# The last mixture's gate per half, its rows kept by expert and its first block by a 0/1 product; both mixtures' closing additions on two engines and an early first down product

## The chip, the cores and the metric

The kernel runs on one core of one Trainium2 chip. The metric is the device time of one execution, in microseconds (us). All arrays are float32 unless a line says otherwise.

## The reference

1024 tokens (32 x 32) of width 256 pass through four layers; each layer adds cross attention, attention and a feed-forward part, each of the layer-normed tokens. The change touches the feed-forward parts of the last two layers, both mixtures of eight experts of which every token takes two. The last one, cut:

```python
gates = softmax(x @ Wg + bg)
_, top_idx = top_k(gates, 2)
mask = one_hot(top_idx, 8).sum(axis=-2)
g = gates * mask
g = g / maximum(sum(abs(g)), 1e-12)
h = gelu(einsum('btd,edh->bteh', x, W1) + b1)      # 256 -> 1024
eo = einsum('bteh,ehd->bted', h, W2) + b2          # 1024 -> 256
return einsum('bte,bted->btd', g, eo)
```

The one before it, the capacity mixture, uses relu and gives each expert at most 160 tokens, the first in token order that chose it.

## The kernel before, in words

`program` (3284) runs the parts as stages one after another, with a barrier of all engines between two. The tokens stay in SBUF as `core.x`, 8 tiles of 128 tokens. Each engine has its own instruction stream and executes it in order; waits on semaphores are written out by hand, and that order is what this change is about. DMAs are issued by SP (most), ACT (its own queue) and POOL (indirect ones).

**The scan** (`stage_scan`, 1835) is the stage ahead of the capacity mixture. At its start SP issues its own loads and then `cw.sp` (2170): it fills the capacity mixture's DRAM arrays `moecap_xin` and `moecap_acc` with neutral rows from the input `nobody` and loads the weights of three experts.

**The capacity mixture** (`stage_moe_capacity`, 2276). `Norm` (74) normalizes in two halves of four tiles; PE turns tiles, ACT copies them to `xnT`. `TopTwo` (2177) computes the two largest gates of a half: PE's logits, twelve small DVE steps each waiting for the one before it (`Chain`, 61), and on PE the rank of each token within its expert (`rank`, 2221, bf16 products of the 0/1 mask with an upper triangle and with ones). The local `slots(h)` (2491) turns ranks into row numbers; POOL scatters the rows of the half to `moecap_xin` (L2364). The first expert doesn't wait for the scatter: DVE builds a 0/1 matrix (L2520, `onehot`), and PE multiplies the tokens with it (`dispatch`, L2387). Experts then go through `turn_x` (L2397), `up` (L2407), ACT's `relu` (L2473), `down` (L2417) and `turn_y` (L2428); in the loop before, the order on PE is up(0), turn_x(1), up(1), turn_x(2), down(0), up(2), ... Results go by POOL's indirect DMA to `moecap_acc` (L2370). At the end SP and ACT fetch both contributions of each tile (`bring`, 2325), and DVE adds share times contribution to `core.x`, two operations for each of eight tiles (L2556).

**The last attention** (`stage_attn3`, in `stage_one_head`, 1354). Its SP calls `ew.sp` (2577): first the whole of `moe_xin` is filled from `nobody` (L2578, 2944 rows), then the 16 MB of the last mixture's weights follow (L2580, L2581).

**The last mixture** (`stage_moe`, 2584). SP issues the small loads (2657 to 2663); ACT waits for all of them before its first copy. `Gate` (2065) works on all eight tiles at once: logits (L2094), softmax, `max` and `max_index` per tile, mask, weights. DVE then sums the masks (L2807), PE forms ranks (L2703 to L2705), and DVE computes how many blocks of 128 rows each expert needs, where each expert's rows begin, and the row of each token (L2816 to L2828). Rows are packed: expert e begins at the block where expert e - 1 ends, and 23 blocks cover every case. POOL scatters 16 times 128 rows to `moe_xin` (L2686). Meanwhile DVE builds the table `expert_u` of the expert of each block, PE turns the weights of the tokens (L2708) and multiplies them with `b2` (L2714), and DVE adds this to `core.x` (L2843).

The loop over blocks: SP loads block n (L2669) into one of two buffers `x_slots`; for n of 2 and more it first waits until block n - 2 is turned and its row numbers are copied (`row_ready`, L2668). `expert_of` (2642) reads the expert's number from SBUF into a register. PE's iteration n is turn_x(n + 1) (L2723), up(n) (L2735, in two halves), down(n - 1) (L2745). DVE's iteration n is prepare(n + 1) (b1 of the expert, L2849, and the block's row numbers, L2851), weights(n + 1) (two copies of W1's halves to `w1_now`, L2859, each after the half of up(n) that used the place), taken(n - 1) (L2865). ACT applies gelu (L2789), POOL writes results to `moe_acc` (L2691). At the end `bring` (L2653), sixteen DVE additions (L2881), and eight stores of the tiles (L2674). A line on DVE, before:

```python
for n in range(BLOCKS + 1):
    if n + 1 < BLOCKS:
        prepare(n + 1)
        weights(n + 1)
    if n:
        taken(n - 1)
```

Of the kernel before, what the change touches and what calls it, by code (L numbers as in the profile page):

```python
# [6 lines left out]
ALU = mybir.AluOpType  # L7
# [7 lines left out]
P = 128  # L15
# [1819 lines left out]
def stage_scan(core, cw):  # L1835
# [11 lines left out]
    with ExitStack() as ctx:  # L1847
# [44 lines left out]
        def _(sp):  # L1892
# [9 lines left out]
            cw.sp(sp)  # L1902

# [161 lines left out]
class Gate:  # L2065


    def __init__(self, st, experts, wg, bg, logits):
        self.core, self.E, self.wg_dram, self.bg_dram, self.logits = st.core, experts, wg, bg, logits
        full = [P, TILES, experts]  # L2070
        self.wg, self.bg = st.sb("gate_w", [P, CD, experts]), st.sb("gate_b", [P, experts])
        self.number = st.sb("gate_number", [P, experts])
        self.sub, self.probs, self.mask = st.sb("gate_sub", full), st.sb("gate_probs", full), st.sb("gate_mask", full)
        self.second, self.weight = st.sb("gate_second", full), st.sb("gate_weight", full)
        self.most, self.total = st.sb("gate_most", [P, TILES]), st.sb("gate_total", [P, TILES])
        self.top, self.index = st.sb("gate_top", [P, TILES, 8]), st.sb("gate_index", [P, TILES, 8], U32)
        self.place = st.sb("gate_place", [P, TILES, 8])
        self.loaded = st.sem("gate_loaded")
        self.logits_done, self.sub_ready = st.sem("gate_logits_done"), st.sem("gate_sub_ready")
        self.exp_ready, self.ready = st.sem("gate_exp_ready"), st.sem("gate_ready")  # L2080

    def sp(self, sp):
        sp.dma_start(self.wg[:, :, :], self.wg_dram.rearrange("(c p) e -> p c e", p=P)).then_inc(self.loaded, 16)  # L2083
        sp.dma_start(self.bg[:, :], self.bg_dram.partition_broadcast(P)).then_inc(self.loaded, 16)
        sp.dma_start(self.number[:, :], self.core.dram["number"][0:self.E].partition_broadcast(P)).then_inc(self.loaded, 16)

    def pe(self, pe):

        core, nc = self.core, self.core.nc
        pe.wait_ge(self.loaded, 48)  # L2090
        for t in range(TILES):
            out = self.logits[:, t * self.E:(t + 1) * self.E]
            for c in range(CD):
                mm = nc.tensor.matmul(out, core.xnT[:, c, t * P:(t + 1) * P], self.wg[:, c, :], start=(c == 0), stop=(c == CD - 1))  # L2094
        mm.then_inc(self.logits_done, 1)

    def act(self, act):
        act.wait_ge(self.sub_ready, 1)
        self.core.nc.scalar.activation(self.probs[:, :, :], self.sub[:, :, :], ACT.Exp).then_inc(self.exp_ready, 1)

    def dve(self, dve, step):
        nc, full = self.core.nc, [P, TILES, self.E]
        by_token = lambda a: a.unsqueeze(2).broadcast_to(full)
        dve.wait_ge(self.loaded, 48)
        dve.wait_ge(self.logits_done, 1)
        step(nc.vector.tensor_tensor(self.sub[:, :, :], self.logits.rearrange("p (t e) -> p t e", t=TILES),
                                     self.bg[:, :].unsqueeze(1).broadcast_to(full), ALU.add))
        step(nc.vector.tensor_reduce(self.most[:, :], self.sub[:, :, :], AX.X, ALU.max))
        nc.vector.tensor_tensor(self.sub[:, :, :], self.sub[:, :, :], by_token(self.most[:, :]), ALU.subtract).then_inc(self.sub_ready, 1)
        dve.wait_ge(self.exp_ready, 1)  # L2110
        step(nc.vector.tensor_reduce(self.total[:, :], self.probs[:, :, :], AX.X, ALU.add))
        step(nc.vector.reciprocal(self.total[:, :], self.total[:, :]))
        step(nc.vector.tensor_tensor(self.probs[:, :, :], self.probs[:, :, :], by_token(self.total[:, :]), ALU.mult))
        for t in range(TILES):
            step(nc.vector.max(self.top[:, t, :], self.probs[:, t, :]))  # L2115
        for t in range(TILES):
            step(nc.vector.max_index(self.index[:, t, :], self.top[:, t, :], self.probs[:, t, :]))  # L2117
        step(nc.vector.tensor_copy(self.place[:, :, :], self.index[:, :, :]))
        number = self.number[:, :].unsqueeze(1).broadcast_to(full)
        step(nc.vector.tensor_tensor(self.mask[:, :, :], number, by_token(self.place[:, :, 0]), ALU.is_equal))  # L2120
        step(nc.vector.tensor_tensor(self.second[:, :, :], number, by_token(self.place[:, :, 1]), ALU.is_equal))
        step(nc.vector.tensor_tensor(self.mask[:, :, :], self.mask[:, :, :], self.second[:, :, :], ALU.add))
        step(nc.vector.tensor_tensor(self.weight[:, :, :], self.probs[:, :, :], self.mask[:, :, :], ALU.mult))
        step(nc.vector.tensor_reduce(self.total[:, :], self.weight[:, :, :], AX.X, ALU.add))
# [3 lines left out]
        dve.sem_inc(self.ready, 1)  # L2128

# [1249 lines left out]
```

## Time and profile before

| | us |
|---|---|
| median of 3 runs | 2022.66 (2016.35 to 2028.9) |
| profiled execution | 2018.47 |
| its span in the profile | 2016.6 |
| PE busy | 1633.3 (81%) |
| DVE busy | 1173.3 (58%) |
| ACT busy | 867.7 (43%) |
| POOL busy | 711.4 (35%) |

PE is TensorE's products, PEld its weight loads (they overlap), DVE VectorE, ACT ScalarE, POOL GpSimd, SPq the queue of SyncE. Busy shares are averages over stages with different limits. In timelines a row is: start in us from the span's start, duration in us, engine, line, operation, written tensor, read tensors, shapes, count; in square brackets the idle time of the engine ahead of it and what ended that. The granted clock of TensorE is a share of full speed (1.00 is 2.4 GHz, 0.50 is 1.2 GHz).

### The profile page before, as it was taken

The page shows a single profiled execution, that of the slowest core. Times are in us where ns is not written, and L with a number is a line of the kernel's source. Part 1 is how long each engine was busy: PE and PEld are TensorE (multiplying, and loading weights), DVE is VectorE, ACT ScalarE, POOL GpSimd, SP SyncE. Part 2 cuts the span into 40 slices and gives each one's busy share as a digit, 9 for nine tenths or more (in the row PEclk, how much of TensorE's full clock was granted, in tenths as well). Part 3 has the DMA queues.
Part 4 walks back from the last instruction along what each step waited for, and adds up shares of the span by engine and source line. Part 5 has one row for each costly group of instructions (what it writes and reads, how often), then busy time and mean ns, then how long its engine had stood idle before and what let it go on. Part 6 is the DMA issues. An engine that isn't in the chain of part 4 may idle for free. (4 is left out here: it accounts for less than half of the span.)

```text
span 2016.6 us, 36051 instructions
## 1 busy us (share of the span) xinstructions
PE 1633.3 (81%) x12690; PEld 1402.0 (70%) x12690; DVE 1173.3 (58%) x3187; ACT 867.7 (43%) x2475; POOL 711.4 (35%) x780
## 2 busy tenths in 40 slices
PE   6999998650785999977999999699595388757996
PEld 6988997330465999946899889456494266546996
DVE  5666665688774888835666666289413565442222
ACT  4666664114543888812666666200131133112332
POOL 7655552541116999713000000177312211112111
PEclk9999999885896999987999999799697588858998
DMA  8444441010004333205222222520362210931112
GB/s 249 149 148 148 149 148 67 29 39 5 0 1 132 130 134 133 94 16 169 75 93 93 93 93 75 165 95 1 91 202 62 68 52 28 320 119 56 38 38 81
DMA packets 120795, 195.52 MB, mean 97 GB/s; under 512 B 17672, under 2 KB 87408, under 8 KB 120272
## 3 DMA queue, kind: packets, MB, share of 16 engines
q1 hardware_dynamic: 113504, 181.32, 27.3%
q0 software_dynamic: 3408, 8.54, 1.2%
q10 hardware_dynamic: 3712, 3.41, 0.6%
q8 instruction: 103, 1.69, 0.3%
q14 instruction: 68, 0.56, 0.1%
HBM read 154.16 MB, written 45.52 MB: 99 GB/s over the span
## 5 line engine op out<-in xcount | busy, mean ns | idle before, releaser
L672 DVE TENSOR_SCALAR xattn_oT<-bank,xattn_last 128x256 f32<-128x256 f32 x256 | 111.7, 478 | 100.1 <-PE bank L512 100.1
L592 ACT ACTIVATE xattn_probs<-bank,xattn_negmax 128x257 f32<-128x257 f32 x256 | 124.2, 485 | 57.8 <-DVE xattn_negmax L653 57.8
L653 DVE TENSOR_REDUCE xattn_negmax<-bank 128x1 f32<-128x257 f32 x256 | 108.0, 422 | 63.0 <-PE bank L485 61.3
L597 ACT ACTIVATE xattn_probs<-xattn_probs,xattn_rsum 128x257 f32<-128x257 f32 x256 | 131.9, 515 | 1.4 <-DVE xattn_rsum L657 1.4
L832 POOL TENSOR_SCALAR xattn_probs<-xattn_probs,xattn_rsum 128x257 f32<-128x257 f32 x128 | 119.9, 937 | 22.9 <-DVE xattn_rsum L1067 22.7
L1907 POOL MEMSET scan_decay<- 128x64 f32 x1 | 0.2, 214 | 337.1 <-POOLq L51 337.1
L603 ACT CAST xattn_probsT_hi<-bank 128x256 fp32r<-128x256 f32 x256 | 95.7, 374 | 40.4 <-PE bank L492 36.7
L662 DVE TENSOR_TENSOR xattn_probsT_lo<-bank,xattn_probsT_hi 128x256 fp32r<-128x256 f32 x256 | 104.9, 410 | 8.3 <-ACT xattn_probsT_hi L603 7.2
L492 PE MATMUL bank<-ident,xattn_probs 128*128 128x128 f32 x512 | 103.6, 285 | 2.5 <-ACT xattn_probs L597 2.0
L136 PE MATMUL bank<-ident,xn 128*128 128x128 f32 x144 | 32.6, 406 | 90.0 <-DVE xn L112 90.0
L481 PE MATMUL bank<-xattn_ctxT,xattn_qk_hi 128*128 128x258 f32 x256 | 93.6, 366 | 0.5 <-DVE xattn_qk L649 0.5
L136 PEld LDWEIGHTS bank<-ident,xn 128*128 128x128 f32 x144 | 26.8, 211 | 95.6 <-DVE xn L112 95.2
L507 PE MATMUL bank<-xattn_probsT_hi,xattn_ctxN 128*128 128x256 f32 x256 | 85.2, 333 | 5.0 <-DVE xattn_oT L672 3.4
L1920 POOL TENSOR_TENSOR scan_product<-scan_state,scan_qT 128x512 f32<-128x512 f32 x64 | 75.7, 1183 | 36.6 <-DVE scan_state L2057 36.2
L2735 PE MATMUL bank<-moe_xinT,moe_w_now 128*128 128x128 f32 x736 | 87.6, 278 | 0.3 <-DVE moe_w_now L2859 0.3
L2735 PEld LDWEIGHTS bank<-moe_xinT,moe_w_now 128*128 128x128 f32 x736 | 85.6, 195 | 0.7 <-ACT moe_xinT L2779 0.6
L402 POOL TENSOR_SCALAR xattn_ctxT<-xattn_rawT 128x514 fp32r<-128x514 f32 x32 | 48.4, 1511 | 102.9 <-issue 101.9
L463 PE MATMUL bank<-xattn_qT,xattn_wk 64*128 64x128 f32 x1024 | 73.3, 283 | 12.8 <-DVE xattn_qT L638 10.0
L2745 PE MATMUL bank<-moe_w,moe_hT 128*128 x368 | 83.1, 379 | 0.0
L2057 DVE TENSOR_TENSOR_SCAN scan_state<-bank,scan_decay 128x264 f32<-128x264 f32 x128 | 81.3, 688 | 1.3
L528 PE MATMUL bank<-xattn_oT,xattn_wv 128*64 128x128 f32 x1024 | 70.7, 282 | 10.0 <-issue 7.6
L463 PEld LDWEIGHTS bank<-xattn_qT,xattn_wk 64*128 64x128 f32 x1024 | 62.2, 187 | 21.9 <-issue 12.6
(500 smaller groups left out, 5426.1 us busy)
## 6 DMA issues: line engine op xcount, KB each, us to landing
xattn_ctxT<-ctx_partsT SPq DMA_DIRECT2D x64, 516.0 KB, 3.6
xattn_ctxN<-ctx_partsN SPq DMA_DIRECT2D x64, 384.0 KB, 3.1
ctx_partsT<-xattn_ctxT SPq DMA_DIRECT2D x32, 516.0 KB, 3.0
moe_w<-in_L_ffn_W SPq DMA_DIRECT2D x16, 1024.0 KB, 13.9
ctx_partsN<-xattn_ctxN SPq DMA_DIRECT2D x32, 384.0 KB, 3.9
moecap_w_early<-in_L_ffn_w SPq DMA_DIRECT2D x10, 1024.0 KB, 12.7
xattn_rawN<-in_ctx SPq DMA_DIRECT2D x32, 192.0 KB
moecap_w_late<-in_L_ffn_w SPq DMA_DIRECT2D x6, 1024.0 KB, 7.5
```

Source lines behind the costliest of these rows:

```text
L463: mm = nc.tensor.matmul(bank[:, k * P:(k + 1) * P], wk_s[r, h // 2, g % 2 * P:(g % 2 + 1) * P], qT[r, h // 2, :], start=True, stop=True, t ...
L481: nc.tensor.matmul(out, unit(qk1[0]), part(0, 0), start=True, stop=False)
L492: mm = nc.tensor.transpose(TB[n % 2][:, c * P:(c + 1) * P], probs[:, n % RING, c * P:(c + 1) * P], core.ident[:, :])
L507: nc.tensor.matmul(OB[:, 0:2 * P], first_hi(c), hi[:, c], start=(c == 0), stop=False)
L592: nc.scalar.activation(probs[:, n % RING, :], SB[n % 2][:, 0:KV], ACT.Exp, bias=negmax[:, n % RING:n % RING + 1], accum_out=psum[:, n % RI ...
L597: nc.scalar.mul(probs[:, n % RING, :], probs[:, n % RING, :], rsum[:, n % RING:n % RING + 1]).then_inc(norm_ready, 1)
L603: nc.scalar.copy(probsT[0][:, n // 2 % PAIRS, :, n % 2, :], TB[n % 2][:, 0:2 * P].rearrange("p (c n) -> p c n", c=2)).then_inc(probsT_hi_r ...
L653: nc.vector.tensor_reduce(negmax[:, n % RING:n % RING + 1], SB[n % 2][:, 0:KV], AX.X, ALU.max, negate=True).then_inc(negmax_ready, 1)
L662: nc.vector.tensor_tensor(lo, TB[n % 2][:, 0:2 * P].rearrange("p (c n) -> p c n", c=2), hi, ALU.subtract).then_inc(probsT_ready, 1)
L672: nc.vector.tensor_scalar(oT[k][:, heads, b, :], by_head(OB[:, k * 2 * P:(k + 1) * 2 * P]), last[:, k, j * PER_TILE + b:j * PER_TILE + b + ...
L832: nc.gpsimd.tensor_scalar(probs[:, n % RING, :], probs[:, n % RING, :], rsum[:, n % RING:n % RING + 1], None, ALU.mult).then_inc(norm_read ...
L2735: mm = nc.tensor.matmul(H[n % 2][k][:, f * P:(f + 1) * P], w1_now[:, c, at:at + P], xinT[:, n % 2, c, :], start=(c == 0), stop=(c == CD - 1))
```

## The change

In the scan SP issues one more DMA, `er.sp`: it fills all of `moe_xin`, which now has a region of 1024 rows for each expert (9088 rows instead of 2944). The fill in `ew.sp` goes. A token's row is its rank in the expert plus 1024 times the expert, so it doesn't depend on how full the others are; a second table `block_row_u` gives the first row of each block, and SP reads from it. The last mixture uses `TopTwo` in halves and scatters in halves; its first block (expert 0) comes from a 0/1 product; down(0) and the b2 shares stand behind up(0). In the capacity mixture down(0) stands behind up(0). In both, ACT scales and POOL adds three of the eight closing tiles. `class Gate` is removed. The diff, cut:

```diff
+BY_POOL = (0, 3, 6)
+BY_DVE = tuple(t for t in range(TILES) if t not in BY_POOL)
...
     def rank(self, pe, h, out, count=None):
...
+        if count is not None:
+            for t in range(TILES):
+                mm = nc.tensor.matmul(count, self.up_to_b[:, 1, :], self.mask[:, t, :], start=(t == 0), stop=(t == TILES - 1))
```

The capacity mixture on PE:

```diff
             for n in range(E + 2):
                 if n < E:
                     up(n)
+                if n == 0:
+                    down(0)
                 if n + 1 < E:
                     turn_x(n + 1)
                 if n >= 2:
                     turn_y(n - 2)
-                if 1 <= n <= E:
+                if 2 <= n <= E:
                     down(n - 1)
```

Both mixtures, the ends of ACT, POOL and DVE, and the fill of `moe_xin`:

```diff
+            act.wait_ge(shares_ready, 1)
+            for t in BY_POOL:
+                act.wait_ge(brought[t], TOP * 16)
+                for k in range(TOP):
+                    nc.scalar.mul(mine[k][:, t, :], mine[k][:, t, :], share[:, k, t:t + 1]).then_inc(scaled, 1)
...
+            for n, t in enumerate(BY_POOL):
+                for k in range(TOP):
+                    pool.wait_ge(scaled, n * TOP + k + 1)
+                    if k:
+                        pool.wait_ge(pool_added, n * TOP + k)
+                    nc.gpsimd.tensor_tensor(core.x[:, t, :], core.x[:, t, :], mine[k][:, t, :], ALU.add).then_inc(pool_added, 1)
...
-            for t in range(TILES):
+            for n, t in enumerate(BY_DVE):
...
+class ExpertRows:
+    def sp(self, sp):
+        sp.dma_start(self.core.moe_xin, self.core.dram["nobody"]).then_inc(self.core.moe_cleared, 16)
...
 class ExpertWeights:
     def sp(self, sp):
-        sp.dma_start(self.xin, self.d["nobody"]).then_inc(self.cleared, 16)
```

The last mixture on SP:

```diff
+        def row_of(eng, n):
+            return eng.value_load(block_row_u[0:1, n:n + 1], min_val=0, max_val=xin.shape[0] - P) if n else 0
...
-            sp.dma_start(up_to[:, :, :], d["up_to"]).then_inc(loaded, 16)
+            sp.dma_start(place[:, :], d["number"][1:P + 1].partition_broadcast(P)).then_inc(loaded, 16)
...
+            sp.wait_ge(experts_ready, 1)
             sp.wait_ge(scattered, TILES * TOP * 16)
             for n in range(BLOCKS):
                 if n >= XS:
                     sp.wait_ge(x_turned, n - XS + 1)
                     sp.wait_ge(row_ready, n - XS + 1)
-                sp.dma_start(x_slots[:, n % XS, :], xin[n * P:(n + 1) * P, :]).then_inc(x_loaded[n % XS], 16)
+                sp.dma_start(x_slots[:, n % XS, :], xin[bass.ds(row_of(sp, n), P), :]).then_inc(x_loaded[n % XS], 16)
```

The last mixture on PE (`shares_of_b2` holds the turns of the weights and the b2 products, which stood ahead of the loop before):

```diff
             def up(n):
                 pe.wait_ge(xT_ready, n + 1)
+                if n == 1:
+                    pe.wait_ge(b2_added, TILES // 2)
...
+            dispatch()
+            pe.wait_ge(ew.loaded, E * 32)
+            up(0)
+            down(0)
+            shares_of_b2()
             pe.wait_ge(experts_ready, 1)
-            pe.wait_ge(b2_added, TILES // 2)
-            pe.wait_ge(ew.loaded, E * 32)
-            turn_x(0)
-            for n in range(BLOCKS + 1):
+            turn_x(1)
+            for n in range(1, BLOCKS + 1):
                 if n + 1 < BLOCKS:
                     turn_x(n + 1)
                 if n < BLOCKS:
                     up(n)
-                if n:
+                if n >= 2:
                     down(n - 1)
```

The last mixture on DVE (`slots(h)` waits for the ranks of the half, adds `begins`, multiplies with the two picks, sums, casts to `slot_u`, signals `slots_ready` and forms `in_first`, 6 steps):

```diff
+            for h in range(2):
+                gate.dve(dve, step, h)
+                slots(h)
+            nc.vector.tensor_tensor(onehot, in_first[:, :].unsqueeze(2).broadcast_to(shape), place[:, :].unsqueeze(1).broadcast_to(shape),
+                                    ALU.is_equal).then_inc(onehot_ready, 1)
...
             prepare(0)
             weights(0)
+            tables()
+            weights_of_tokens()
             for n in range(BLOCKS + 1):
                 if n + 1 < BLOCKS:
                     prepare(n + 1)
                     weights(n + 1)
+                if n == 0:
+                    add_b2()
+                if n < BLOCKS:
+                    row(n)
                 if n:
                     taken(n - 1)
```

`row(n)` holds the two lines that leave `prepare(n)`: the wait for the block's rows and the copy of their row numbers (`row_ready`). `tables()` is the arithmetic for `expert_u` and `block_row_u` (15 steps), `weights_of_tokens()` the shares and the token weights (6 steps). On ACT the order is turned_x(0), gelu(0), the copies of the turned weights, turned_x(1), and then turned_x(n + 1), gelu(n) as before. POOL issues eight scatters after `slots_ready` 1 and eight after 2.

## Rows read from the trace of the kernel before

**Rows 1.** Stretch: length, busy us (count) of five engines, PE clock, DMA share, GB/s

```profile
1831.00:1994.00 163.00, 162.74 (x1124) 152.90 (x1124) 45.17 (x111) 61.87 (x207) 20.13 (x21) 0.99 0.11 35
```

**Rows 2.** Chain of waits that ended last, last mixture (start, us, what)

```profile
1777.44 3.85 DMA moe_b<-in_L_ffn_b
...
1825.21 2.43 DMA moe_xin<-moe_x,moe_slot_u
...
1827.66 2.00 DMA moe_x_slots<-moe_xin
...
1830.44 0.70 DVE moe_w_now L2859
...
1836.85 3.57 PE bank L2735 x32
```

**Rows 3.** DMA issues: count, KB each, median us to landing

```profile
moe_xin<-in_nobody SPq DMA_DIRECT2D x1, 2955.5 KB, 11.7
```

**Rows 4.** A stretch (columns as in rows 1) and the first issue of the last mixture

```profile
1765.00:1770.00 5.00, 4.49 (x23) 3.38 (x21) 2.52 (x6) 1.88 (x6) 0.00 (x0) 1.00 1.06 379
...
1770.80 1.87 SPq L2083 DMA_DIRECT2D moe_gate_w<-in_L_ffn_Wg  x1
```

**Rows 5.** Timeline of the capacity mixture (start, us, engine, line, op)

```profile
1422.61 0.60 SPq L2338 DMA_DIRECT2D moecap_b<-in_L_ffn_b_cols  x1
...
1425.56 0.30 ACT L2446 COPY moecap_x<-moecap_rows 128x8 f32<-128x8 f32 x2 [107.42 <-DMA moecap_b<-in_L_ffn_b_cols]
...
1437.58 1.22 POOL L2364 DMA_INDIRECT moecap_xin<-moecap_x,moecap_slot_u  x1 [11.36 <-issue]
...
1443.04 1.49 DVE L2520 TENSOR_TENSOR xnT<-moecap_chosen,moecap_place 128x1280 f32<-128x1280 f32 x1
...
1444.58 6.67 PE L2387 MATMUL bank<-xnT,moecap_x 128*128 128x160 f32 x32 [4.61 <-DVE xnT L2520]
...
1451.87 4.58 PE L2407 MATMUL bank<-moecap_xinT,moecap_w_early 128*128 128x160 f32 x32 [0.61 <-ACT moecap_xinT L2466]
...
1463.77 0.80 PE L2397 MATMUL bank<-ident,moecap_x_slots 80*128 80x80 f32 x4 [7.32 <-DMA moecap_x_slots<-moecap_xin]
...
1465.13 6.63 PE L2407 MATMUL bank<-moecap_xinT,moecap_w_early 128*128 128x160 f32 x32 [0.56 <-issue]
...
1476.26 4.51 PE L2407 MATMUL bank<-moecap_xinT,moecap_w_early 128*128 128x160 f32 x32
```

**Rows 6.** Timeline of one block of the last mixture

```profile
1967.14 3.74 PE L2735 MATMUL bank<-moe_xinT,moe_w_now 128*128 128x128 f32 x32
...
1967.98 0.15 DVE L2851 CAST moe_row_u<-moe_x_slots 128x1 uint32<-128x1 f32 x1
...
1968.20 0.32 SPq L2669 DMA_DIRECT2D moe_x_slots<-moe_xin  x1
...
1970.72 3.62 PE L2745 MATMUL bank<-moe_w,moe_hT 128*128 x16
...
1971.03 0.69 DVE L2859 COPY moe_w_now<-moe_w 128x1024 f32 x1 [1.09 <-PE bank L2735]
...
1974.17 0.38 PE L2723 MATMUL bank<-ident,moe_x_slots 128*128 128x128 f32 x2
```

**Rows 7.** Value loads, line 2643: duration ns min/median/max

```profile
L2643 DVEq TENSOR_LOAD <-moe_expert_u x46: 298/304/552, 1810.8 to 1982.4; - x46
```

**Rows 8.** Stretches when PE ran dry at the end, columns as in rows 1

```profile
1999.00:2000.00 1.00, 0.31 (x2) 0.00 (x0) 0.42 (x1) 0.00 (x0) 0.00 (x0) 1.00 0.01 0
...
2001.00:2002.00 1.00, 0.00 (x0) 0.00 (x0) 0.00 (x0) 0.00 (x0) 0.49 (x1) 0.89 0.00 0
```

**Rows 9.** Closing additions: last one on DVE; an addition of this shape on POOL

```profile
2013.29 0.48 DVE L2881 SCALAR_TENSOR_TENSOR x<-xnT,moe_share,x 128x256 f32<-128x256 f32 x1
...
L3018 POOL TENSOR_TENSOR x<-x,xattn_bo x8: 724/728/734, 1598.7 to 1603.5; 128x256 f32<-128x256 f32 x8
```

More of the change, by code:

```diff
@@ L2061, in _ @@
                 add(t, bank[t - len(OUT)])
[L2065 to L2090, printed above, removed]
-        for t in range(TILES):
[L2092 to L2124, printed above, removed]
-        step(nc.vector.tensor_scalar(self.total[:, :], self.total[:, :], 1e-12, None, ALU.max))
-        step(nc.vector.reciprocal(self.total[:, :], self.total[:, :]))
-        step(nc.vector.tensor_tensor(self.weight[:, :, :], self.weight[:, :, :], by_token(self.total[:, :]), ALU.mult))
-        dve.sem_inc(self.ready, 1)
@@ L2220, in pe, with rank @@
         mm.then_inc(self.logits_done, 1)
-    def rank(self, pe, h, out):
+    def rank(self, pe, h, out, count=None):
         nc, E, first = self.core.nc, self.E, h * 4
@@ new lines, in _, with dispatch @@
+            for h in range(2):
+                gate.rank(pe, h, RANK[h], COUNT if h else None)
+            def dispatch():
+                pe.wait_ge(onehot_ready, 1)
+                for c in range(CD):
+                    for t in range(TILES):
+                        mm = nc.tensor.matmul(XT[0][:, c * P:(c + 1) * P], xk[0][:, t, c * P:(c + 1) * P], onehot[:, t, :],
+                                              start=(t == 0), stop=(t == TILES - 1))
+                mm.then_inc(x_turned, 1)
@@ L2797, in _ @@
             bring(act, 1)
+            act.wait_ge(shares_ready, 1)
+            for t in BY_POOL:
+                act.wait_ge(brought[t], TOP * 16)
+                for k in range(TOP):
+                    nc.scalar.mul(mine[k][:, t, :], mine[k][:, t, :], share[:, k, t:t + 1]).then_inc(scaled, 1)
         @block.vector
@@ L2802, in _ @@
             step = Chain(dve, steps)
-            gate.dve(dve, step)
-            tiles = [P, TILES, E]
-            step(nc.vector.memset(before[:, 0, :], 0.0))
-            for t in range(TILES):
-                add = nc.vector.tensor_tensor(before[:, t + 1, :], before[:, t, :], gate.mask[:, t, :], ALU.add)
-                if t < TILES - 1:
-                    step(add)
-            add.then_inc(before_ready, 1)
-            step(nc.vector.tensor_tensor(first[:, :, :], gate.mask[:, :, :], gate.second[:, :, :], ALU.subtract))
@@ new lines, in weights_of_tokens, with add_b2 @@
+            def weights_of_tokens():
+                gate.shares(dve, step)
+                dve.sem_inc(shares_ready, 1)
+                for k in range(TOP):
+                    step(nc.vector.tensor_tensor(chosen[:, k, :, :], gate.picked[:, k, :, :], share[:, k, :].unsqueeze(2).broadcast_to([P, TILES, E]), ALU.mult))
+                nc.vector.tensor_tensor(weight[:, :, :], chosen[:, 0, :, :], chosen[:, 1, :, :], ALU.add).then_inc(weight_ready, 1)
+            def add_b2():
+                for k in range(TILES // 2):
+                    dve.wait_ge(b2_done, k + 1)
+                    both = core.x[:, 2 * k:2 * k + 2, :].rearrange("p t n -> p (t n)")
+                    nc.vector.tensor_tensor(both, both, bank[k], ALU.add).then_inc(b2_added, 1)
```

211 lines of the change are left out of this document (122 added, 89 removed).

## Prediction

> **What bounds the kernel now.** I read the busy shares of the page first, then the stretches, then the chain of waits of the last mixture, then the timelines of both mixtures. The change touches only the two mixtures, one DMA in the scan, and nothing of the other 1,600 us. In the main loop of the last mixture PE is busy 162.7 of 163 us at a granted clock of 0.99 [rows 1]: there only less PE work, or a new wait of PE, counts. Ahead of the loop PE is idle, and the chain shows what it waits for: the last small load (issued at 1777.44, landed 3.85 us later), the gate, sixteen scatters of rows into DRAM by POOL, the last of them from 1825.21, and the load of the first block's rows, 2.00 us [rows 2]. The second block's up product starts at 1836.85 [rows 2]; I call that point U.
>
> **Clearing moved into the scan.** The DMA of 2955.5 KB that stood ahead of the weights in the last attention goes [rows 3]. That queue ran full at 379 GB/s [rows 4], so the weights end 2955.5 KB / 379 GB/s = 8.0 us sooner, and the mixture's first small issue, 1.87 us long [rows 4], no longer stands behind them. In the scan the clearing grows to 9088 rows of 257 floats, 9.3 MB, 25 us of a queue that has nothing to carry there after the early weights, some 90 us before the scan ends: nothing there pays.
>
> **Head of the last mixture.** ACT begins at 1781.3 before. After: some 2.3 us less in the first two issues, one issue more (`place`), and a landing as in the capacity mixture, 1425.56 - 1422.61 = 2.95 us [rows 5]: 1778.4. From there the capacity mixture shows the new gate, which is the same class: its one-hot starts 1443.04 - 1425.56 = 17.5 us later [rows 5]. Here a half's slots take 6 steps of 0.22 us instead of 14, but wait for the rank products, which now carry the count too: I take 1.0 us off per half and 0.25 for a step left out between. The one-hot has 1024 elements against 1280 (1.49 us), so 1.2. Dispatch starts at 1778.4 + 16.5 = 1794.9 and takes 6.5 (6.67 for wider products, paced by the weight loads [rows 5]). In the capacity mixture the next up product follows 0.6 us later and runs 4.58 us where one at the low clock takes 6.63 [rows 5]; so up(0) here runs at full clock, 3.6 us, to 1805.6. Gelu with its table load ends at 1807.4, early down(0) at 1811.05 (3.62 us [rows 6]).
>
> Then the b2 shares, which used to lie under the scatters, stand on PE's path: turns and two copies 1.9 us, sixteen products (3.5 us at the full clock, by their like in down, and twice that at the low one), the last addition 0.8: 1817.3. The scatters are no longer in the way: POOL starts 12.0 us after ACT in the capacity mixture [rows 5], 1.1 sooner here, at 1789.3, its last at 1808.3 and the first rows at 1812.8.
>
> What is late next is the row copy. The change takes `row(n)` out of `prepare(n)` and puts it behind `weights(n + 1)`, and `row(0)` behind the b2 additions. SP waits for row n - 2 before it loads block n (two buffers), and PE turns block n before up(n - 1). So up(1) waits for: row(0) at 1817.4, SP, 2.0 us of load, the turn: 1820.6. **U moves from 1836.85 to 1820.6, a gain of 16.2 us.** Bounds: 12 (b2 products at the low clock) to 18.
>
> **The loop.** Before, one block takes 7.25 us of PE (20 periods from U), and the next rows are asked for at 1968.20, 1.06 us after up(n) starts at 1967.14 [rows 6]; they are needed at 1974.17. After, they are asked for behind the second half's weight copy, which starts only when up(n) is through: 1971.03 + 0.69 [rows 6]. The chain from up(n)'s start s: copy done s + 4.6; the row copy starts s + 4.5, and before SP issues 0.22 us behind that start [rows 6]; now SP also reads a block's row number from SBUF. A value load shows 0.30 us in the middle and 0.55 at most [rows 7]; with its address arithmetic DVE's next operation starts 1830.44 - 1829.66 = 0.78 us after the rows landed, 0.15 of it the row copy [rows 2, 6], so 0.63, and part of the load lay under the copy. No SP row shows it; between 0.4 and 1.0 I take 0.7, nearest to DVE's. Issue at s + 5.4, landed s + 7.45, turn and next up s + 7.95. The period grows from 7.25 to 7.95: 0.7 us, for the 20 turns that stand ahead of up(2) to up(21): **-14 us** (0.35 to 1.0 each: -7 to -20). The 3.46 us of down(0) taken out of the loop bring nothing: its place between up(1) and up(2) is empty now, and the rows are late there too.
>
> The page "DMA: Bandwidth & Descriptors" of the Trainium skill, in its section on latency and other measured facts, puts the floor of such a register load at about 600 ns; the trace's 304 ns disagrees [rows 7]. By the page SP would need 0.3 us more a block, 6 us in all. The sum here goes by the trace.
>
> **Clock.** After PE's last product at 1999.3 the granted clock stands for 2.6 us and then falls (0.89 in 2001 to 2002) [rows 8]. PE's gap ahead of up(1) is about 3.4 us and the one after it 3.9, so both may fall; an up product at the low clock costs 1.8 to 2.1 us more (6.63 against 4.51 to 4.58 [rows 5]). I take -2.3, between 0 and -4. The 0.7 us gaps of the loop are too short for it.
>
> **Capacity mixture, early down(0).** Before, PE ends up(0) at 1456.45 and idles until the turn at 1463.77 [rows 5]. Down(0) (4.5 us) now fills this gap; what stays idle, about 2.2 us, is under the 2.6 that stood the clock above, so up(1) takes 4.5 us and not 6.63. Its relu, the load that ACT issues next and the copy of block 2 put up(2) at 1471.1 instead of 1476.26 [rows 5]: **5.2 us** gained. If the clock falls, 3.1. Weights 6 are asked for sooner and share the queue with ACT's row loads; these have some 5 us to land.
>
> **Closing additions, both mixtures.** DVE keeps five tiles of eight, at 0.48 us an addition, two each; ACT scales three tiles (0.4 us an operation, as its copies of this width), POOL adds them at 0.73 [rows 9]. DVE alone worked 7.4 us, but the data land over 6 of them, so the last tile counts: 0.9 on ACT, 1.5 on POOL. I take 0.8 us of gain in each mixture, between -0.5 and 1.5.
>
> **Sum**, against the profiled execution's own time of 2018.47 (span 2016.6): 5.2 + 0.8 + 16.2 - 14 - 2.3 + 0.8 = 6.7 us, so 2011.8. The median of the three runs shown, 2022.66, lies 4.2 above that execution; the forecast for a median is 2016.
>
> **Rivals.** (a) *The forecast*: a stall of 0.45 to 0.85 us a block; 2009 to 2023, 2016 as the likeliest; chance 0.50. (b) *A short chain and a clock that holds*: SP's load takes 0.35 us with its address, a stall of 0.3 x 20 = 6 and no clock loss: 6.8 + 16.2 - 6 = 17, 2005.7; for it speaks the 0.30 of the load alone [rows 7]; 0.20. (c) *No stall*: the change then does what moving the scatters off the path promises, 6.8 + 16.2 + 3.5 = 26.5, 1996; it needs the rows 0.7 us earlier than my chain gives, against it every wait in the code; 0.08. (d) *SP's load at its longest*, 0.55 [rows 7]: stall 0.95 x 20 = 19, so 2021; the Trainium skill's page points the same way; 0.13. (e) *Slower*: same place, the request for the rows of block n + 2 behind up(n). It decides from a stall of (6.8 + 16.2 - 2.3) / 20 = 1.03 us a block. Load and address at 1.2 us and rows landing 0.2 later give 1.4 x 20 = 28, with a clock loss of 4: 23 - 32 = -9, so 2032; for it speaks that nothing on SP was measured; 0.07. (f) *The loop's gaps let the clock fall again and again*: 1.8 x 20 = 36 more, 2052; 0.02.
>
> **Chances.** One per cent, 20 us, is about what this kernel's runs (2016 to 2029) can tell from no change. Faster by over 1% (below 2002.4): (c) and a part of (b), 0.13. Slower by over 1%: (f) and the end of (e), 0.03. Within: 0.84. The range 2002 to 2027 leaves out (c), most of (e), and (f).
>
> **What would show it.** In the trace after: PE's clearest sign is the period of the last mixture's loop, 7.95 us and not 7.25, with waits of the turn for the DMA of the rows; a first up(1) 16 us earlier; the last small load landing near 1778 by this trace's clock; in the capacity mixture a down product between up(0) and the first turn, and the next up in 4.5 us. A period of 7.25 would refute the main step, a period above 8.3 would make the kernel slower.

## The result, and the profile after

| | before | after |
|---|---|---|
| median of 11 runs each, us | 2021.40 | 2032.78 |
| lowest to highest | 2016.35 to 2031.82 | 2026.60 to 2041.98 |
| ratio, 95% interval | | 1.0052 [1.0029, 1.0075] |
| profiled execution (span) | 2018.47 (2016.6) | 2036.77 (2035.0) |

(PE is TensorE, DVE VectorE, ACT ScalarE, POOL GpSimd.) The change makes the kernel half a per cent slower, by 11 us; 2016 was forecast, and the measured time lies outside the range of 2002 to 2027. The profiled executions differ by 18.3 us. Cut at the first load of each stage, 14.0 of them arise in the last mixture (245.8 to 259.8 us), 2.8 in the capacity mixture (139.1 to 141.9), and 2.3 ahead of the scan, where the two kernels are the same; the stages between give 0.7 back.

The main loop, in stretches of the changed kernel (columns as in rows 1):

```profile
1860.00:2000.00 140.00, 133.78 (x896) 120.06 (x896) 36.85 (x90) 47.87 (x162) 16.82 (x18) 1.00 0.12 35
```

PE is busy 133.8 of 140 us where it was busy 162.7 of 163 [rows 1], at the full clock: it now waits once a block. One block, in the timeline (the answer to rows 6; the SP row joins two issues, and the window cuts the first product off the first row: this up starts at 1967.67):

```profile
1967.78 3.62 PE L2729 MATMUL bank<-moe_xinT,moe_w_now 128*128 128x128 f32 x31
...
1971.55 0.69 DVE L2885 COPY moe_w_now<-moe_w 128x1024 f32 x1 [1.09 <-PE bank L2729]
...
1972.16 0.15 DVE L2877 CAST moe_row_u<-moe_x_slots 128x1 uint32<-128x1 f32 x1
1973.10 8.17 SPq L2639 DMA_DIRECT2D moe_x_slots<-moe_xin  x2
...
1975.22 0.44 PE L2715 MATMUL bank<-ident,moe_x_slots 128*128 128x128 f32 x2 [0.36 <-DMA moe_x_slots<-moe_xin]
...
1975.50 3.74 PE L2729 MATMUL bank<-moe_xinT,moe_w_now 128*128 128x128 f32 x32
```

The row copy stands behind the weight copy, SP's request 0.94 us behind the row copy's start (0.22 before [rows 6]), and the turn waits for the load. The period is 7.7 to 7.9 us (once 8.1), not 7.25. SP's part, by its line (min/median/max ns):

```profile
L2612 SPq TENSOR_LOAD <-moe_block_row_u x22: 263/266/494, 1815.1 to 1995.8; - x22
L2612 SPq FUSED_REGOPS  x22: 152/152/182, 1815.6 to 1996.1; - x22
```

The chain of waits in the head of the last mixture (the answer to rows 2):

```profile
1779.45 2.66 DMA moe_b<-in_L_ffn_b
...
1799.37 6.54 PE bank L2691 x32
1805.90 10.28 issue
1816.18 6.66 PE bank L2729 x32
...
1824.06 3.72 PE bank L2739 x16
...
1829.45 4.33 PE bank L2706 x16
1833.80 0.32 DVE x L2867
...
1835.36 2.07 DMA moe_x_slots<-moe_xin
...
1838.16 5.76 PE bank L2729 x32
```

The last small load lands 6.9 us after the stage's first issue instead of 10.5, 3.6 us sooner where 2.9 were forecast, and the dispatch begins 24.2 us after it, where the forecast's walk has 24.1. Then there is a hole of 10.28 us between the dispatch (L2691) and up(0) (L2729). It is called "issue", so the profile has nothing that PE waited for. up(0) then takes 6.66 us, the time of a product at the low clock (the granted clock was 0.56 from 1816 to 1823). The second block's up, the point U of the prediction, starts 62.95 us after the stage's start; it was 66.05. The same hole is in the capacity mixture (answer to rows 5); the releaser of ScalarE's copy (in brackets) is unknown to the profile, "remote":

```profile
1446.19 6.50 PE L2332 MATMUL bank<-xnT,moecap_x 128*128 128x160 f32 x32 [4.54 <-issue]
...
1457.87 0.43 ACT L2413 COPY moecap_xinT<-bank 128x320 f32<-128x320 f32 x1 [16.34 <-remote]
1458.44 7.17 PE L2352 MATMUL bank<-moecap_xinT,moecap_w_early 128*128 128x160 f32 x32 [5.75 <-ACT moecap_xinT L2413]
...
1466.10 4.61 PE L2362 MATMUL bank<-moecap_hT,moecap_w_early 128*128 128x160 f32 x32 [0.48 <-ACT moecap_hT L2420]
```

The dispatch's last product ends at 1452.7, ScalarE copies at 1457.87, 5.2 us later. In the kernel before the same copy followed at once (1451.25 to 1451.30). In both mixtures GpSimd issues its scatters of rows during the hole.

### The profile page after: what moved, and what is told of

Its sections match the earlier page's. It is cut to its first block and busy times, and to the rows that moved or that the text cites. A ratio compares the mean times of both kernels' runs of the same rounds, so it can differ in the third digit from the quotient of the medians.

```text
span 2035.0 us, 36249 instructions
## 1 busy us (share of the span) xinstructions
PE 1651.8 (81%) x12734; PEld 1413.0 (69%) x12734; DVE 1174.6 (58%) x3166; ACT 873.2 (43%) x2488; POOL 721.1 (35%) x795
## 5 line engine op out<-in xcount | busy, mean ns | idle before, releaser
L2729 PE MATMUL bank<-moe_xinT,moe_w_now 128*128 128x128 f32 x736 | 93.3, 289 | 10.3 <-issue 10.3
L2729 PEld LDWEIGHTS bank<-moe_xinT,moe_w_now 128*128 128x128 f32 x736 | 91.6, 206 | 10.5 <-issue 10.4
L2668 POOL DMA_INDIRECT moe_acc<-moe_y_slots,moe_row_u x23 | 22.1, 962 | 183.5 <-DVE moe_y_slots L2891 176.7
L2739 PE MATMUL bank<-moe_w,moe_hT 128*128 (+1 forms) x368 | 83.2, 379 | 1.2 <-ACT moe_hT L2790 1.2
L2885 DVE COPY moe_w_now<-moe_w 128x1024 f32 (+1 forms) x46 | 32.0, 697 | 85.5 <-PE bank L2729 85.5
## 6 DMA issues: line engine op xcount, KB each, us to landing
moe_w<-in_L_ffn_W SPq DMA_DIRECT2D x16, 1024.0 KB, 13.1
moe_xin<-in_nobody SPq DMA_DIRECT2D x1, 9123.5 KB, 39.5
```

Source lines behind the costliest of these rows:

```text
L2729: mm = nc.tensor.matmul(H[n % 2][k][:, f * P:(f + 1) * P], w1_now[:, c, at:at + P], xinT[:, n % 2, c, :], start=(c == 0), stop=(c == CD - 1))
L2739: mm = nc.tensor.matmul(Y[n % 2][:, 0:D], hT[:, n % 2, f, :], w2[:, bass.ds(e, 1), f, :].rearrange("p a f -> p (a f)"), start=(f == 0), st ...
```

## The experiments

Three theories, besides the forecast's own: (1) the row request behind the weights sets the loop; (2) something makes PE's results reach the other engines late in the head; (3) the closing additions on GpSimd cost instead of gain. Runs e1 to e8 were made on one chip, e9 to e11 on a second, e12 to e15 on a third (of the first comparison the chip isn't on record); ratios are to the kernel before on the same chip.

**e1, the changed kernel again.** 

> The changed kernel, once more, for a second trace. In its first trace ScalarE's copy of the dispatched first block starts 5.2 us after the last dispatch product in the capacity mixture and 9.8 us after it in the last one, with nothing in the trace that releases it. Theory A: the delay belongs to the kernel (its order, its code); then both gaps are there again, within 0.5 us of 5.2 and 9.8, and the time is 2033. Theory B: it is an accident of the one execution; then one or both are under 1 us, and if both are, up(0) runs at the full clock and the profiled time is about 2037 - 15 - 6 = 2016.

2026.92. Neither theory: the delay is 3.2 us in the capacity mixture, and in the last mixture it has moved. ScalarE's copy follows the dispatch at once, but then up(0) seems to end by 1807, while its two halves are answered late (timeline; the DVE row's releaser is a stale one of the earlier stage):

```profile
1802.68 0.37 ACT L2780 COPY moe_xinT<-bank 128x256 f32<-128x256 f32 x1 [10.03 <-issue]
...
1803.16 3.81 PE L2729 MATMUL bank<-moe_xinT,moe_w_now 128*128 128x128 f32 x32 [0.51 <-issue]
...
1808.90 0.69 DVE L2885 COPY moe_w_now<-moe_w 128x1024 f32 x1 [4.79 <-DMA xnT<-moecap_acc]
...
1813.15 1.14 ACT L2790 ACTIVATE moe_hT<-bank,moe_b_now 128x128 f32<-128x128 f32 x4 [1.58 <-DMA xnT<-moecap_acc]
```

VectorE may copy the next weights after the first half, some 2 us after the product's start; it does so after 5.7, and ScalarE's second half after 10.0. Two engines see it at once, so it is PE's side that is late: its signals, or the products themselves (the ends of PE's records are modelled; the last section comes back to this). U is at 57.0.

**e2, row copies early.**

```diff
                 if n + 1 < BLOCKS:
                     prepare(n + 1)
+                    if n:
+                        row(n + 1)
                     weights(n + 1)
                 if n == 0:
                     add_b2()
-                if n < BLOCKS:
-                    row(n)
+                    row(0)
+                    row(1)
```

> The row copies of the last mixture one block ahead of the weight copies, as before the change, all else as changed. Theory 1 (the loop's period is the chain row copy, SP's request, load, turn, copy, up): the request of block n+1 no longer stands behind the weights of block n, PE doesn't wait for a load, the period goes from 7.78 back to 7.25, and the time falls by 20 x 0.55 = 11 to 16 us, to about 2019. Rival (the period has risen for another reason, a lower clock or the added products' buffers): the period stays at 7.7 to 7.8 and the time within 3 us of the changed kernel's 2033. The two delays of ScalarE's first copies should stay if they belong to the code.

2012.95, ratio 0.9936 [0.9908, 0.9963]. Period 7.25 for every block, PE never idle in the loop (stretch, columns as above):

```profile
1850.00:1965.00 115.00, 115.00 (x797) 107.74 (x796) 32.05 (x80) 41.47 (x142) 15.34 (x16) 1.00 0.13 37
```

The last mixture takes 236.3 us against 252.4 in e1, 16.2 less. Theory 1 holds.

**e3, SP's value load ahead of its waits.**

```diff
             for n in range(BLOCKS):
+                at = row_of(sp, n)
                 if n >= XS:
...
-                sp.dma_start(x_slots[:, n % XS, :], xin[bass.ds(row_of(sp, n), P), :])...
+                sp.dma_start(x_slots[:, n % XS, :], xin[bass.ds(at, P), :])...
```

> SP reads the row number of the next block (a value load of 0.27 us, with 0.17 us of arithmetic and a check behind it) ahead of its two waits, all else as changed. Theory 1 (the chain of the row sets the loop's period): this load and what hangs on it leave the chain, the period falls by 0.4 to 0.7, to 7.1 to 7.4, and the time by 8 to 14 us, to 2019 to 2025. Rival (the chain isn't the bound): period 7.7 to 7.8 and a time of 2033, within 3.

2016.67, ratio 0.9953 [0.9934, 0.9972]; period 7.24 to 7.31. The read with its address took 0.72 us of the chain (0.94 against 0.22 from the row copy to the request), and the stall was 0.56 a block (7.81 - 7.25), so without it PE no longer waits in the steady loop. It still waits 3.2 us for the rows ahead of up(2), and the last mixture takes 241.1 us, 11.4 less than in e1, where e2 gained 16.2. Both halves of theory 1, the order behind the weights and the read on SP, are needed for the stall.

**e4, all closing additions on VectorE.**

```diff
-BY_POOL = (0, 3, 6)
+BY_POOL = ()
...
-            for t in BY_DVE[0:1] + BY_POOL[0:1] + BY_DVE[1:3] + ...
+            for t in BY_DVE:
```

> All closing additions of both mixtures on VectorE again (the list for GpSimd empty, stores in VectorE's order), all else as changed. Theory 3 (GpSimd's additions lengthen VectorE's from 0.48 to 0.83 to 1.0 us, and GpSimd ends late at the barrier): VectorE's sixteen additions of 0.51 take 8.2 us in each mixture, the same as or less than the 7.5 to 8.5 of the two engines now, the barrier after the capacity mixture falls from 3.8 to 1.4 us, and the time falls by 2 to 5 us. Rival (the split gives what it was worked out to give, a little under 1 us in each mixture): the time rises by 1 to 3 us.

2025.51, ratio 0.9991 [0.9967, 1.0015]. The period stays at 7.7 to 7.9. The capacity mixture takes 137.1 us against 140.1, 140.3 and 140.2 in e1 to e3, the last mixture 251.4 against 252.4. Theory 3 holds, mainly in the capacity mixture. It rests on the stages: the changed kernel has only the one run of e1 on this chip, so the times don't decide it.

**e5, the kernel before again.** 

> The kernel before, once more, for a second trace. In its first trace ScalarE's copy of the dispatched first block of the capacity mixture started 0.05 us after the last dispatch product (1451.25 to 1451.30), with GpSimd's scatters running beside it; in five traces of changed kernels it starts 2.2 to 5.2 us after it. Theory A (the delay belongs to the changed kernel): 0.05 us again. Theory B (any kernel can meet it): a gap of 2 us or more here too. The distance from the first load of the capacity mixture to the first of the next stage is 139.1 in the first trace; by A it is there again within 1.

2023.25; the delay is there in the kernel before too, 6.8 us (timeline, capacity mixture):

```profile
1443.77 6.35 PE L2387 MATMUL bank<-xnT,moecap_x 128*128 128x160 f32 x32 [4.54 <-issue]
...
1456.89 0.43 ACT L2466 COPY moecap_xinT<-bank 128x320 f32<-128x320 f32 x1 [17.77 <-remote]
```

Theory B: the changed kernel did not bring the delay. Its stage takes 143.0 us, 4 more than in the first trace. In its last mixture nothing is lost (247.9 us, as in e13 with 248.0). There PE's last product, of `b2`, ends under the fourth of the sixteen scatters, VectorE's addition follows at once, and the other twelve scatters have no PE work beside them (timeline):

```profile
1813.66 0.96 POOL L2686 DMA_INDIRECT moe_xin<-moe_x,moe_slot_u  x1 [0.30 <-issue]
1814.45 0.69 DVE L2843 TENSOR_TENSOR x<-x,bank 128x512 f32<-128x512 f32 x1 [1.02 <-PE bank L2714]
```

**e6, the clearing back ahead of the weights.** The DMA of 9123.5 KB moves from the scan's SP program to `ExpertWeights.sp`. 

> The clearing of the last mixture's rows back to the place before its weights (9.1 MB there instead of 3.0), all else as changed. Theory C (the fill in the scan, which lies 60 us ahead of the capacity mixture, has nothing to do with PE's late signals): ScalarE's copy in the capacity mixture is 2 to 5 us behind the dispatch as in the changed kernel, and the time is its 2027 to 2033, or a few us more if the larger fill is late for the scatters. Rival D (moving the fill brought the delay): the gap is 0.05 us, and the time is about 3 us lower.

2064.15, ratio 1.0195 [1.0161, 1.0230]. The delay is there (8.7 us), so the fill has nothing to do with it. What I expected of the time was wrong: the larger fill ahead of the weights makes them late, and the last mixture's first load is issued at 1791.26 instead of 1772.67 (e1). The stage of the scan is as long with the fill as without (138.5 against 137.8 here, 138.7 before): there it is free, and with 9.1 MB this is the only cheap place of the two.

**e7, down(0) of the capacity mixture late.**

```diff
-                if n == 0:
-                    down(0)
...
-                if 2 <= n <= E:
+                if 1 <= n <= E:
                     down(n - 1)
```

> The first down product of the capacity mixture back behind the turn of block 1 and up(1), all else as changed. The stage takes 140.1 us in the second trace of the changed kernel (first load to first load of the next stage). By my sum the early product is worth 5.2 us: the stage would take 145 and the time would rise by 5. Rival: the early product gives nothing because ScalarE's loads of the rows stand behind its relu: 140, and the same time. Whether the delay of ScalarE's copy (2 to 5 us) goes too tells whether the order of the products brings it.

2042.28, ratio 1.0084 [1.0055, 1.0114]. The delay is 6.8 us here as well. The stage takes 145.25 us; with the product early and the same delay (e8) 142.31: the early product is worth 2.9. The time is 15 us above e1's one run, which this doesn't explain: of the 14.5 us between the two traces 5.2 lie in this stage, 5.4 between the mixtures, where nothing was changed, and 3.0 in the last mixture.

**e8, the last mixture's scatters behind gelu(0).**

```diff
+            pool.wait_ge(gelu_done, FCH)
             for h, half in enumerate(Norm.HALVES):
                 pool.wait_ge(slots_ready, h + 1)
```

> GpSimd's scatters of the last mixture wait for the last gelu of block 0, so that dispatch, up(0) and gelu(0) have no scatter beside them; the scatters then start about 15 us later than they do, so the whole should take about 10 us longer than the changed kernel: only the head is read. Theory E (PE's signals come late while scatters run): up(0)'s two halves are signalled 1.9 and 3.8 us after its start (it was 5.7 and 10.0 in four traces), gelu(0) starts then, and w1 is copied for block 1 then. Rival F (PE's signals come late for another reason: its code, its clock): they take 5.7 and 10.0 us again.

2043.29. In one execution both mixtures can be read: the first with its scatters beside the products, the second without (timelines):

```profile
1441.98 6.34 PE L2332 MATMUL bank<-xnT,moecap_x 128*128 128x160 f32 x32 [4.54 <-DVE xnT L2472]
...
1455.10 0.43 ACT L2413 COPY moecap_xinT<-bank 128x320 f32<-128x320 f32 x1 [17.77 <-remote]
...
1808.84 3.81 PE L2730 MATMUL bank<-moe_xinT,moe_w_now 128*128 128x128 f32 x32 [0.51 <-issue]
...
1811.01 0.69 DVE L2886 COPY moe_w_now<-moe_w 128x1024 f32 x1 [1.68 <-PE bank L2730]
...
1812.79 0.69 DVE L2886 COPY moe_w_now<-moe_w 128x1024 f32 x1 [1.09 <-PE bank L2730]
```

6.8 us late beside scatters; without them VectorE gets its signals 2.2 and 3.9 us after up(0)'s start. Theory E holds for this chip.

**e9 to e11, combinations.** e9 is e2 and e4 together. e10 is e2 with the `b2` products behind the last block:

```diff
             up(0)
-            down(0)
-            shares_of_b2()
             pe.wait_ge(experts_ready, 1)
             turn_x(1)
-            for n in range(1, BLOCKS + 1):
+            up(1)
+            turn_x(2)
+            down(0)
+            for n in range(2, BLOCKS + 1):
...
+            shares_of_b2()
```

with the turned weights in `w1_now`, and ScalarE's copies and VectorE's `add_b2()` behind their loops. e11 is all three.

> Row copies early and all closing additions on VectorE together. Alone they gave 2013 (period 7.25) and 2025.5 against the changed kernel's 2033. If the two effects are separate (loop and closings), they add: the early rows' 20 us and 2 to 3 us in each mixture for the closings, 2007 to 2011. Rival (the closings' part of the second run was scatter of the stages between, which moved by 3 to 8 us with TensorE's clock): 2013 again, within 3.

> As the run with the early row copies, and the products of the second biases moved behind the last block (the weights' turns, ScalarE's copies, the products, VectorE's four additions), where VectorE waits 6.8 us for the fetched rows; up(1) stands right behind the turn of block 1, down(0) behind it. Theory 4 (the head of the last mixture is held by PE's own path, down(0) in the low clock 5.8, the biases' turns and products 5.5, the request for block 2's rows behind VectorE's additions 3.7, all behind PE's late signals): the rows of block 1 land at about 40.3 us after the stage's start plus 2, so up(1) starts 44 after it instead of 57, and with one more down product in the loop (3.5) the time falls by 9 against the 2013 of the early rows: 2004. Rival (the rows are not there earlier, or the biases' work in the tail is not hidden): up(1) at 50 or later, or the tail 4 us longer: 2009 to 2013.

> Early row copies, the biases' products in the tail, and all closing additions on VectorE. If all three are separate: the 2004 expected of the one before less the 4 to 5 us of the closings, 2000. Rival: in the tail VectorE has the four additions of the biases and sixteen of its own, and the rows fetched are there before it has done the first four; then it is 2 to 3 us longer than without, and the time is 2002 to 2004.

1998.67, 2000.22 and 1999.53; ratios 0.9886 [0.9855, 0.9918], 0.9915 [0.9886, 0.9943] and 0.9903 [0.9872, 0.9934]: one group. The times expected were worked out from the first chip. e9 came out 8 us under the lowest time expected of it; here the kernel before is faster too (2019.23 against 2024.5), and no trace shows a late signal. U stands at 51.3 in e9 and at 44.8 and 45.2 in e10 and e11, where 44 was expected of e10. In e11 the first closing addition starts 4.0 us after the fetches are issued and in e9 2.7: the four additions of `b2` are not quite hidden, as its rival said.

**e12 to e15, side by side on a third chip**: the changed kernel, the kernel before, e9's and e11's.

> The changed kernel again, timed with the candidates on one chip. If TensorE's signals are prompt in this trace (ScalarE's copy of the dispatched block within 0.1 us of the last dispatch product, in both mixtures), then up(1) should start about 50 us after the stage's start instead of 57 to 63, the capacity mixture should take 137 instead of 140, and the time should stand at or just under the kernel before (ratio 0.998 to 1.002). If they are late by 3 us or more, the ratio should be 1.004 to 1.008 again.

> The kernel before again, for a trace beside the changed kernel's on one chip. If lateness belongs to the chip or the time and not to the kernel, its ScalarE copy in the capacity mixture is late here when the changed kernel's is, and prompt when that is prompt.

> Early row copies and all closing additions on VectorE, again, beside the changed kernel. By the parts (the loop 11 to 15 us of period, the closings 2 to 3 in each mixture) it should lie 17 to 22 us under the changed kernel whatever the signals do, as it keeps the same head. Rival (its 0.9886 on the other chip was owed to prompt signals there): 12 us or less under the changed kernel of this call.

> As the one before, with the biases' products in the tail. With prompt signals the two were equal (0.9886 and 0.9903). With late signals the head of this one has less on TensorE's path (no turns, no bias products, down(0) behind up(1)), so it should be 3 to 8 us faster than the other; with prompt ones equal within 3 us.

| | median | ratio | stage, capacity | U | stage, last |
|---|---|---|---|---|---|
| e12, changed | 2018.62 | 0.9996 [0.9975, 1.0016] | 138.6 | 48.6 | 245.3 |
| e13, before (one run) | 2018.88 | | 138.6 | 68.2 | 248.0 |
| e14, rows early, additions on VectorE | 1998.66 | 0.9902 [0.9886, 0.9919] | 136.0 | 51.4 | 230.3 |
| e15, and `b2` in the tail | 1993.42 | 0.9876 [0.9858, 0.9893] | 136.2 | 44.7 | 228.2 |

All signals are prompt in these four traces, in both kernels. There the changed kernel is as fast as the one before (its capacity mixture takes 138.6 us, where I expected 137), and its chain through the head has no hole:

```profile
1790.88 5.38 PE bank L2691 x32
...
1796.77 2.04 PE bank L2729 x16
...
1802.69 3.72 PE bank L2739 x16
...
1808.08 4.12 PE bank L2706 x16
...
1813.77 2.11 DMA moe_x_slots<-moe_xin
```

In e15 the chain of the head runs through the scatters and the first load, not through PE:

```profile
1802.51 2.65 DMA moe_xin<-moe_x,moe_slot_u
...
1806.63 2.02 DMA moe_x_slots<-moe_xin
...
1809.90 6.00 PE bank L2728 x32
```

e15's kernel beats both, by 1.2% [1.1, 1.4] over the one before. It is 5 us under e14 where I expected at most 3; the intervals touch, and e9 and e11 stood the other way round, so the place of the `b2` products is not settled. The traces speak against it: of the 7.4 us between the executions of e14 and e15, 7.0 lie between the mixtures, where the two are the same and the granted clock was lower in e14 (0.59 from 1700 to 1730 us, against 0.77 in e15's like stretch, 1702 to 1732), and 2.1 in the last mixture. Early rows and VectorE's additions are settled: 19 us (0.94%) between e12 and e14.

The closing additions of the capacity mixture, e12 (two engines; timeline):

```profile
1539.51 3.67 SPq L2269 DMA_DIRECT2D xn<-moecap_acc  x8
...
1548.38 0.95 DVE L2509 SCALAR_TENSOR_TENSOR x<-xn,moecap_share,x 128x256 f32<-128x256 f32 x1
1549.19 0.72 POOL L2316 TENSOR_TENSOR x<-x,xnT 128x256 f32<-128x256 f32 x1
1549.36 0.83 DVE L2509 SCALAR_TENSOR_TENSOR x<-xnT,moecap_share,x 128x256 f32<-128x256 f32 x1
...
1553.95 1.34 DVE L3218 MEMSET xattn_raw<- 22x1536 f32 x1 [3.76 <-PEq L51]
```

and e14 (VectorE alone):

```profile
1537.97 3.67 SPq L2269 DMA_DIRECT2D xn<-moecap_acc  x8
...
1548.05 0.48 DVE L2509 SCALAR_TENSOR_TENSOR x<-xnT,moecap_share,x 128x256 f32<-128x256 f32 x1
...
1549.91 1.34 DVE L3220 MEMSET xattn_raw<- 22x1536 f32 x1 [1.38 <-PEq L51]
```

From the fetches' issue to the last addition's end it is 10.7 us with two engines and 10.6 with one: an addition of VectorE takes 0.83 to 0.95 us instead of 0.48 while GpSimd adds. Then the barrier into the next stage takes 3.8 us instead of 1.4. GpSimd's last addition ends at 1549.91, ahead of VectorE's, so it is not late work. Why the barrier is longer after GpSimd has added, the profile doesn't show.

## Why the prediction was wrong, step by step

- **The loop: the mechanism right, the sum right by luck.** Forecast -14 for the row chain and -2.3 for the clock. From U to up(21) it is 160.75 us against 144.95, -15.8. Two errors cancel: the stall is 0.56 a block, 11 over 20, and the other 4.6, beyond the bound of 4, lie at the first two blocks, whose up products take 5.8 us instead of 3.7, at the low clock (0.62 granted from 1838 to 1844). By the block shown, the request goes out at s + 5.4 (as forecast), SP's part is 0.72 (0.7 forecast), and the next up starts at s + 7.8 (7.95): only turn to up was priced too long, 0.28 us instead of 0.5. The mechanism is shown from both ends by e2 and e3. Rival (d), SP's read at 0.55, did not come: 0.266. Rival (e)'s 2032 is the measured time by accident: it wanted a stall of 1.4 a block.
- **Head of the last mixture, +16.2: this step failed. It was right only where PE's signals are prompt, a hidden condition.** e12: U at 48.6 against 66.05, a gain of 17.4 (19.6 against e13's 68.2). In the profiled execution it was 3.1, in e1 9.0. Up to the dispatch the walk held (24.2 us, 24.1 forecast). The sentence that failed is "so up(0) here runs at full clock, 3.6 us, to 1805.6", and with it the whole walk from the dispatch to down(0). I took it from one trace of the kernel before in which a dispatch stood beside the scatters unharmed [rows 5], and e5 shows that same kernel 6.8 us late at that place. The old order kept PE's work out of the scatters' time; the new one puts dispatch, up(0) and down(0) into it. None of my rivals had this.
- **Capacity mixture, early down(0), +5.2: mis-sized.** Worth 2.9 (e7 against e8), and the fetches leave 2.7 us earlier after the stage's start in e12 than in e13. The choice that failed is that the gap ahead of up(1) keeps the clock: it is 2.8 us in e12, and up(1) takes 6.26 us, at a granted clock of 0.73 over it. The lower bound of 3.1 was the case.
- **Closing additions, +0.8 twice: wrong sign.** About -2.5 in the capacity mixture (13.3 us from the fetches' issue to the next stage in e14, 15.8 in e12); in the last one the way from the last block's turn to the end is 35.3 us in e12 and 35.9 in the profiled execution against 34.8, so -0.5 to -1.1. I priced VectorE's share at 0.48 an addition as if alone [rows 9] and left out the barrier. VectorE's additions lengthen only while GpSimd's run. The Trainium skill's page "SBUF — State Buffer", section "Who interferes with whom", says that a VectorE instruction with two inputs in SBUF contends with a GpSimd instruction that reads SBUF; these additions are of that kind, and the trace agrees, 0.83 to 0.95 us against 0.48. That rule spoke against this change and should have been weighed.
- **Clearing in the scan: right**, nothing to pay, though the DMA takes 39.5 us to land where 25 were worked out (e6 shows what the other place costs).

With prompt signals the terms as measured make 2.7 - 2.5 + 17.4 - 16.3 - 0.5 = +0.8 us gained (16.3 is e12's own loop), and e12's ratio is 0.9996. The forecast was 6.7 gained and the profiled execution lost 18.3, so 25.0 us are to be explained: 13.1 in the head, 8.8 in the capacity mixture (3.3 of them late signals, 141.9 against e12's 138.6, the rest the two mis-sized terms), 1.9 in the last closing and 1.6 outside the mixtures, less 0.5 in the loop.

What late signals cost, by the stages: in the capacity mixture 4.4 us of the kernel before (143.0 in e5, 138.6 in e13) and 1.5 to 3.3 of the changed kernel (e1 and the profiled execution against e12); in the last mixture nothing of the kernel before and 7.1 to 14.5 of the changed kernel. That is enough for the 0.5% of the result, but it is argued and not timed: the changed kernel has no timed comparison on the chip of e1 to e8, its other ten runs of the first comparison have no trace, and the first trace of the kernel before shows prompt signals.

## What to carry to other kernels

A register read that a request needs belongs ahead of the waits of that request, and a small copy that releases the next load belongs ahead of the large one that doesn't: either alone brought the loop back to 7.25 us a block, and the copy's place also the wait ahead of the second block. Before an operation is shared out to GpSimd, look at what it does to VectorE's operations of the same moment and to the barrier behind. And work that is moved beside sixteen software-issued scatters needs more than one trace to be priced; profile the kernel before twice, on two chips if there are two.

## What was not expected of the hardware

On one chip PE's results reached ScalarE and VectorE late while GpSimd issued scatters: in the capacity mixture by 2.2 to 8.7 us in all of e1 to e8, the kernel before among them, and in the last mixture by up to 10.8 (e6). On two other chips, in e9 to e15, never. Without scatters beside them they are prompt in the same execution (e8). In two traces, that of the first comparison and e6, the last mixture's hole lies behind the dispatch, in others behind up(0).

The traces say more on whether the products or the signals are late. In the capacity mixture of the first comparison's trace of the changed kernel:

```profile
1458.44 7.17 PE L2352 MATMUL bank<-moecap_xinT,moecap_w_early 128*128 128x160 f32 x32 [5.75 <-ACT moecap_xinT L2413]
1462.10 1.38 ACT L2420 ACTIVATE moecap_hT<-bank,moecap_b 128x160 f32<-128x160 f32 x4 [3.80 <-PE bank L2352]
```

Each of ScalarE's operations waits for four products of its own. Four products take 1.07 us here by their starts in the trace, and 0.54 in e12, at the full clock, but the first three operations start 0.28 us apart, back to back. So several groups of products were done before the first signal arrived: here the signals were held up and came together. The same traces lack signals of the scatters. Of the 256 landing signals of the capacity mixture's sixteen scatters, 84 to 99 are recorded in e1 to e8 and in the first comparison's trace of the changed kernel, and all 256 in the other eight traces, the ones with prompt signals. The list of DMA issues shows it as a missing time to landing, here that first trace and e12:

```profile
moecap_xin<-moecap_x,moecap_slot_u POOLq DMA_INDIRECT x16
moecap_xin<-moecap_x,moecap_slot_u POOLq DMA_INDIRECT x16, 2.8
```

In the last mixture the count separates them too (71 to 170 against 251 to 256). The medians of the kernel before fit: 2025.2 and 2024.5 us on the chip of e1 to e8, 2019.2 and 2018.3 on the other two. Why signals are held up, whether the missing ones are a cause or a sign of it, and why chips differ, is open; a kernel with the rows scattered by another queue was not tried.
